# A two-stage mixture-of-experts kernel: seven of the 39 expert tiles get fixed widths from 112 down to 16 tokens

## What is computed

```python
def _L0_ffn_ref(hidden_states, Wr, W1, b1, W2, b2):
    x = hidden_states.reshape(b * s, d)
    router_logits = x @ Wr
    router_probs = jax.nn.softmax(router_logits, axis=-1)
    expert_idx = jnp.argmax(router_probs, axis=-1)
    p_max = jnp.max(router_probs, axis=-1, keepdims=True)
    def expert_mlp(w1, bb1, w2, bb2):
        h = jax.nn.gelu(x @ w1 + bb1, approximate=False)
        return h @ w2 + bb2
    outs = jax.vmap(expert_mlp)(W1, b1, W2, b2)
    onehot = jax.nn.one_hot(expert_idx, e, dtype=x.dtype)
    out = p_max * jnp.einsum('te,etd->td', onehot, outs)
...
x = x + 0.5 * _L0_ffn_ref(_layernorm(x), ...)
x = x + _L0_attn_ref(_layernorm(x), ...)      # h = a_disc * h + B_disc @ u; y = Re(C @ h)
x = x + 0.5 * _L0_ffn_ref(_layernorm(x), ...)
```

## Time and profile before

| | before |
|---|---|
| median of 3 runs | 636.2 us (635.69 to 638.94) |
| the profiled execution: its time, its span | 638.26 us, 636.5 us |
| busy: PE, PEld, DVE, ACT, POOL | 89%, 81%, 74%, 66%, 44% of the span |
| chain that ended last: PE, DVE, ACT | 76%, 12%, 4% of the span |
| L1104 (product 1), L1121 to L1123 (product 2) in that chain | 32%, 33% |
| first matmul of `ffn(1)` and of `ffn(2)` | at 99.0 us and at 414.0 us |
| last matmul of each | ends at 319.1 us and at 631.3 us |
| mean granted clock of PE | 0.991 |

### The profile page before, as it was taken

One profiled execution on the slowest core, in us unless ns is written; L12 is line 12 of the kernel. 1 busy time (PEld: TensorE's weight loads), 2 busy tenths in 40 slices (PEclk: granted clock), 3 DMA queues, 4 the chain that ended last, 5 costly groups with the idle time before them and its releaser, 6 DMA issues.

```text
span 636.5 us, 18503 instructions
## 1 busy us (share of the span) xinstructions
PE 565.4 (89%) x6476; PEld 518.6 (81%) x6476; DVE 473.1 (74%) x981; ACT 419.5 (66%) x966; POOL 280.3 (44%) x309
## 2 busy tenths in 40 slices
PE   5992118999998999999998988789999999999996
PEld 5991008999997999999956766689999999999996
DVE  6578995888888888888718997756677666666674
ACT  3697985767766676666625763277666676776662
POOL 0040055555455555554135113346555555555522
PEclk9999999999999999999999998899999999999999
DMA  8999021111121111121063114112111111111210
GB/s 270 368 377 324 5 82 35 52 38 53 40 51 44 39 49 50 50 52 37 19 191 109 66 67 138 49 36 61 38 51 52 50 49 50 47 42 51 44 33 1
DMA packets 34872, 51.93 MB, mean 82 GB/s; under 512 B 6747, under 2 KB 27933, under 8 KB 34528
## 3 DMA queue, kind: packets, MB, share of 16 engines
q1 hardware_dynamic: 24800, 31.93, 14.8%
q0 software_dynamic: 9984, 18.83, 11.0%
HBM read 37.98 MB, written 14.59 MB: 83 GB/s over the span
## 4 chain that ended last, share of the span: by engine, by line
PE 76%; DVE 12%; issue 4%; ACT 4%; DMA 2%; POOL 1%; SPq 0%; POOLq 0%; DVEq 0%; ACTq 0%
PE banks L1104 32%; PE banks L1123 11%; PE banks L1121 11%; PE banks L1122 11%; PE banks L1039 4%; DVE weights_arena L968 3%; PE banks L1080 3%; PE banks L1011 2%; ACT weights_arena L449 2%; DVE weights_arena L965 1%; DVE weights_arena L949 1%; ACT weights_arena L440 1%; DVE weights_arena L633 1%; DVE weights_arena L977 1%; PE banks L1017 1%
## 5 line engine op out<-in xcount | busy, mean ns | idle before, releaser
L523 ACT ACTIVATE weights_arena<-banks,b1t,inv 128x128 f32<-128x128 f32 x624 | 226.7, 469 | 37.5 <-PE banks L1104 37.4
L1104 PE MATMUL banks<-weights_arena 128*128 128x128 f16 x3744 | 222.1, 219 | 3.3 <-DVE weights_arena L825 2.0
L1104 PEld LDWEIGHTS banks<-weights_arena 128*128 x3744 | 215.1, 98 | 6.1 <-issue 5.3
L1123 PE MATMUL banks<-weights_arena 128*128 x624 | 170.1, 273 | 0.0
L1121 PE MATMUL banks<-weights_arena 128*128 x624 | 170.1, 273 | 0.0
L1122 PE MATMUL banks<-weights_arena 128*128 x624 | 170.1, 273 | 0.0
L836 DVE TENSOR_SCALAR weights_arena<-weights_arena,hscale 128x512 f16<-128x512 f32 x156 | 78.2, 501 | 58.1 <-ACT weights_arena L523 57.3
L839 DVE SCALAR_TENSOR_TENSOR weights_arena<-weights_arena,hscale 128x512 f16<-128x512 f32 x156 | 117.2, 752 | 5.6
L508 ACT ACTIVATE weights_arena<-banks,xscale 128x256 f16<-128x256 f32 x78 | 37.1, 476 | 98.0 <-PE banks L1080 95.7
L362 POOL DMA_INDIRECT recf<-records,sorti x78 | 85.5, 1097 | 23.8 <-issue 23.8
L368 POOL DMA_INDIRECT x_after_ffn<-weights_arena,sorti x39 | 40.0, 1025 | 89.6 <-DVE weights_arena L859 82.7
(11 more groups left out here) (201 smaller groups left out, 620.1 us busy)
## 6 DMA issues: line engine op xcount, KB each, us to landing
weights_arena<-L_ffn_W SPq DMA_DIRECT2D x16, 1024.0 KB, 12.6
weights_arena<-x_after_ffn SPq DMA_DIRECT2D x8, 516.0 KB, 7.4
weights_arena<-L_attn_u SPq DMA_DIRECT2D x8, 512.0 KB, 10.1
x_after_ssm<-weights_arena SPq DMA_DIRECT2D x8, 512.0 KB, 2.9
weights_arena<-L_ffn_b SPq DMA_DIRECT2D x2, 1024.0 KB, 5.3
recf<-records,sorti POOLq DMA_INDIRECT x78, 2.7
weights_arena<-L_attn_u,sorti POOLq DMA_INDIRECT x39, 3.2
x_after_ffn<-weights_arena,sorti POOLq DMA_INDIRECT x39, 2.6
```

Of the source, the lines that this page charges most:

```text
L523: last = act.activation(hb[q % 2][:, f, :], src, ACT.Gelu, bias=b1t[:, bass.ds(e * FC + f, 1)], scale=inv1[:, bass.ds(e, 1)])
L1104: last = pe.matmul(acc[:, f * P:(f + 1) * P], weights[wpart * DC + d], xts[q % 2][:, xpart, d, :], start=(n == 0), stop=(n == 5))
L1123: last = pe.matmul(acc, hs[q % 2][:, 1, f, :], high, start=False, stop=(f == FC - 1))
```

## The change

Seven of the 39 tiles, q = 32 to 38, get a fixed width of `width(q) = 16 * (39 - q)`: 112, 96, 80, 64, 48, 32 and 16 tokens. Their transposes, products, gelus, splits, results, gathers and scatters take only so many tokens. They hold the least filled last tiles of the experts, the least filled of all in the last place used. With M tiles in use, the k-th least filled last tile (k from 0) goes to place M - 1 - k if that is 32 or more; the eight experts' gaps add up to 128 (M - 32), so that it always fits. The tiles with 128 rows, the full ones and the fuller last ones, take places 0 to 31 in the experts' order.

To rank them, `route_count` gets more instructions on DVE (the gaps, `key`, a comparison of all pairs, `rank`, `place_of`, `partial`, `limit`, and two tables of tile places against experts). POOL gets `tile_slots`, seven instructions that make of these the number `vid` that the sorted order gave to each place. `route_tiles` compares with `vid_h` instead of a constant list, and so waits for POOL (`vids`). The sum of tiles (`tend`) moves from `route_owners` to `route_count`.

Three things move besides. In phase 2 the first two groups of `route_rows` stand ahead of `route_tiles`. `second_norm` gets its first half in the recurrence's chunk 5. And `turn_tile(1)`, which stood behind `product1(0)`, stands ahead of it in phase 1 and between its halves in phase 2.

```diff
+        def width(q):
+
+            return P if q < NJ else STEP * (NT - q)
...
+            def tile_slots(ph):
+
+                pool.wait_ge(S[ph]["slots"], 2)
+                parts = over_experts[:, NJ:NTE, :]
+                chain.link(pool.tensor_tensor(parts, parts, tend.unsqueeze(1).to_broadcast([P, NTE - NJ, E]), ALU.mult))
+                for n in (4, 2, 1):
+                    chain.link(pool.tensor_tensor(over_experts[:, :, 0:n], over_experts[:, :, 0:n],
+                                                  over_experts[:, :, n:2 * n], ALU.add))
+                pool.tensor_tensor(vid[:, 0:NJ], over_experts[:, 0:NJ, 0], iota_r[:, 0:NJ], ALU.add)
+                chain.link(pool.tensor_scalar(vid[:, NJ:NTE], over_experts[:, NJ:NTE, 0], -1.0, None, ALU.add))
+                pool.tensor_scalar(vid_h, vid, BIG / P, None, ALU.add).then_inc(S[ph]["vids"], 1)
...
+                if c == NC - 3:
+                    pool.wait_ge(s_sq, NC // 2)
+                    second_norm(slice(0, NJ // 2))
             pool.wait_ge(s_sq, NC - 1)
-            second_norm(slice(0, NJ - CT))
+            second_norm(slice(NJ // 2, NJ - CT))
...
-                            last = act.activation(hb[q % 2][:, f, :], src, ACT.Gelu,
+                            last = act.activation(hb[q % 2][:, f, 0:width(q)], src, ACT.Gelu,
...
-                link(dve.tensor_scalar(tend.bitcast(I32), tiles.bitcast(I32), 7, None, ALU.arith_shift_right))
-                link(dve.scalar_tensor_tensor(base, tend.bitcast(I32), float(P), cnt, ALU.mult, ALU.subtract))
-                link(dve.tensor_tensor(total[:, 1:E, 0], total[:, 1:E, 0], base[:, 0:E - 1], ALU.add))
+                link(dve.tensor_scalar(tiles_i.bitcast(I32), tiles.bitcast(I32), 7, None, ALU.arith_shift_right))
+                link(dve.scalar_tensor_tensor(slack, tiles_i.bitcast(I32), float(P), cnt, ALU.mult, ALU.subtract))
+                dve.tensor_copy(tiles, tiles_i.bitcast(I32))
+                link(dve.scalar_tensor_tensor(key, slack, float(E), rev[:], ALU.mult, ALU.add))
+                dve.tensor_tensor(total[:, 1:E, 0], total[:, 1:E, 0], slack[:, 0:E - 1], ALU.add)
+                dve.tensor_tensor_scan(tend, one[:].to_broadcast([P, E]), tiles, 0.0, ALU.mult, ALU.add)
+                larger = view(12288, E, E)
+                link(dve.tensor_tensor(larger, key.unsqueeze(1).to_broadcast([P, E, E]),
+                                       key.unsqueeze(2).to_broadcast([P, E, E]), ALU.is_gt))
+                link(dve.tensor_reduce(rank, larger, AX, ALU.add))
+                dve.tensor_scalar(place_of, rank, -1.0, tend[:, E - 1:E], ALU.mult, ALU.add)
+                link(dve.tensor_scalar(partial, rank, float(NJ), tend[:, E - 1:E], ALU.add, ALU.is_lt))
+                link(dve.tensor_tensor_scan(passed, one[:].to_broadcast([P, E]), partial, -64.0, ALU.mult, ALU.add))
+                link(dve.tensor_tensor(passed, tend, passed, ALU.subtract))
+                link(dve.scalar_tensor_tensor(limit, partial, -64.0, passed, ALU.mult, ALU.add))
...
+                dve.tensor_tensor(over_experts[:, NJ:NTE, :], per_slot(iota_r[:, NJ + 1:NTE + 1], NTE - NJ),
+                                  per_expert(place_of, NTE - NJ), ALU.is_equal).then_inc(s["slots"], 1)
+                dve.tensor_tensor(over_experts[:, 0:NJ, :], per_slot(iota_r[:, 0:NJ], NJ), per_expert(limit, NJ),
+                                  ALU.is_ge).then_inc(s["slots"], 1)
...
+                dve.wait_ge(S[ph]["vids"], 1)
...
             route_count(2)
+            route_places(2)
+            route_rows(2, 0)
+            route_rows(2, 1)
             route_tiles(2)
             route_odds(2)
-            for g in range(NJ // GR):
-                route_rows(2, g)
+            route_rows(2, 2)
+            route_rows(2, 3)
...
-                                        last = pe.matmul(acc[:, f * P:(f + 1) * P], weights[wpart * DC + d],
-                                                         xts[q % 2][:, xpart, d, :], start=(n == 0), stop=(n == 5))
+                                        last = pe.matmul(acc[:, f * P:f * P + n_cols], weights[wpart * DC + d],
+                                                         xts[q % 2][:, xpart, d, 0:n_cols], start=(n == 0), stop=(n == 5))
...
-                            pe.matmul(acc, hs[q % 2][:, 0, f, :], high, start=(f == 0), stop=False)
+                            pe.matmul(acc, hs[q % 2][:, 0, f, of], high, start=(f == 0), stop=False)
...
-                product1(0, w)
-                turn_tile(1)
+                if ph == 1:
+                    turn_tile(1)
+                product1(0, w, meanwhile=1 if ph == 2 else None)
```

90 lines of the change are left out of this document (54 added, 36 removed).

## The result

| | before | after |
|---|---|---|
| median (15 runs each, in turns) | 636.47 us | 630.44 us |
| ratio, 95% interval | | 0.991 (0.9881 to 0.994) |
| the profiled execution: time, span | 638.26, 636.5 us | 628.32, 626.4 us |

What follows compares the result with a forecast made beforehand. Only PE's time was taken to count inside the tile loops, with weight preparation and routing ahead of them; -0.15 - 7.2 - 0.3 + 3.3 - 7.2 - 0.3 = -11.85 us, from 636.2 to 624.3 us, range 620 to 632.

Steps and rivals of the forecast that it cites:

- The end of the second loop: Last scatter of the loop, 16 rows instead of 128: 0.3 us saved, between 0 and 1.
- Product 1: First product of the seven narrow tiles on PE: 7.4 us saved less 0.2 for the sequencer, 7.2 a phase (5.2 to 7.8).
- the two laws: Product 1's matmul price: by width with floor 25 ns, or straight line from 25 to 55.8; saving 7.8 or 7.0 us.
- The turn and product 2: Narrow tiles' transposes and second product on PE: no gain; product 2 keeps 109 ns a matmul and 2.62 us.
- Rivals A and B: Product 1 bound by its loads, 638.7 us (7%); product 2's narrow loads standing ahead of its matmuls, 642.3 us (8%).
- The ranking ahead of the first loop: Added DVE instructions in route_count delay ACT and DVE by 2.0 us, less 0.4 in route_owners: net +1.65 us.
- The start of the first loop: Turning tile 1 before product 1 of tile 0 lets tile 1's product 1 follow at once: -1.8 us.
- The routing of phase 2: Ahead of the second loop: DVE's ranking +2.1 us and its wait for POOL +1.0.
- the wait for POOL: DVE's tile table in phase 2's routing waits for POOL's vids: 0 to 3 us, taken as 1.0.
- PE's clock behind the longer gap: PE's longer idle before phase 2's routing matmuls leaves them slower: 0 to 0.7 us, taken as 0.2.
- The turn in phase 2: Tile 1's turn moved into product 1 of tile 0: gain 0, since norm(2) still waits for its gather.
- C: Rival: POOL holds up phase 2's routing, or the clock stays at 1.2 GHz beyond it: +3 to +6 us, 627 to 630; 15%.

Runs made afterwards that it cites:

- e3: The changed kernel with every gather moving 128 rows again, scatters still narrow; 628.57 us, 0.9841 of the kernel before.
- e7: The changed kernel with all scatters at 128 rows and gathers narrow in phase 2 alone; executed once for its trace, 662.79 us.
- e17: The changed kernel with compute narrow but all gathers and scatters at 128 rows; 621.97 us for 637.72 of the kernel before, 0.9779.
- e18: The kernel before with only the earlier turn of tile 1, no ranking, all widths 128; 0.9947 of the kernel before.
- e10: The changed kernel with compute narrow, all gathers and scatters at 128 rows, on a slower chip; 652.89 us, 0.991 of the kernel before.
- e9: The changed kernel as it is, run again on a slower chip; 663.15 us, 1.0056 of the kernel before (658.76 us).
- e12: Narrow compute, all DMAs 128 rows except the last two tiles' token-row gathers (208 rows fewer); executed once, 656.21 us.
- e5: The changed kernel with compute narrow, all gathers and scatters at 128 rows, on a slower chip; 655.4 us of 659.12, 0.9933.
- e11: The kernel before with only the earlier turn of tile 1, on a slower chip; 0.9998 of the kernel before.

## Why the prediction was wrong, step by step

- **The end of the second loop: the step that failed.** The prediction took 0.3 us off for a scatter of 16 rows, between 0 and 1, and looked at nothing behind it. The landing of the last scatter came 0.06 us sooner; POOL's DRAIN behind it made the end 8.4 us later, and it was the narrow gathers that made the DRAIN long (e3, e7), for which the sum had no term at all. The range of this step held no loss. The trace of before had the row to ask about: a DRAIN of 3.25 us that closes the queue which issued all indirect DMAs, and ends 0.62 us after SP is through. Its price with narrow DMAs wasn't to be had from before. But that they gain 0.3 us, 1 at the most, and that no row shows their bad end, was known, and speaks for leaving them full. e3 and e17 show the rest of the sum without it.
- **Product 1, forecast -7.2 a phase:** -6.74 in both. By the starts, the seven products 1 save 7.3 us (2.68 down to 2.36, 2.04, 1.73, 1.41, 1.30, 1.29, 1.29), close to the middle of the two laws. From start to start the matmuls follow the first of them (49, 42, 36, 30 ns for 112 to 64 columns, then 25.6), and the floor of 25 was near. The rest, 0.6 for the 0.2 taken, is mostly not in product 1: from product 2 of the tile with 112 columns on, the step from its last matmul to what follows takes 0.20 us for 0.11, five times a phase. What lengthens it isn't shown.
- **The turn and product 2, forecast 0:** right, 109 ns a matmul with 32 and with 16 stationary columns. The Trainium skill's TensorE: Matmul & The Clock Gate, Weight-path perf modes, has the fast load of weights only for 128 weights. The trace agrees: a load of 112 columns is recorded at 130 ns, one of 128 at 98; from 112 down the loads get shorter by 6 to 7 ns for every 16 columns, to 90 ns at 16. The 130 ns are more than the 93 ns that the prediction had estimated for 112 columns by its LDWEIGHTS section, and more than the 109 ns between two matmuls, but the loads overlap, one starting every 0.11 us, and stayed beside the matmuls. Rivals A and B have fallen.
- **The ranking ahead of the first loop, +1.65:** +1.69. ACT waits 2.10 us for expert 4's scales (`[2.10 <-DVE wscale L655]`), so there was no slack to hide it.
- **The start of the first loop, -1.8:** -2.0.
- **The routing of phase 2, +3.1:** +2.24. DVE's share, 2.1, was right; the wait for POOL, 0 to 3 and taken as 1.0, is 0. POOL needed 3.07 us for what I had put at 2.0 to 6.1 (389.21 to 392.28), and the cover was 3.4, for the 3.5 worked out. PE's clock behind the longer gap:

```profile
396.00:398.00 2.00, 2.00 (x16) 2.00 (x17) 1.79 (x12) 0.69 (x2) 0.29 (x1) 0.50 0.11 33
398.00:400.00 2.00, 2.00 (x12) 2.00 (x11) 1.11 (x4) 0.00 (x0) 1.69 (x2) 0.50 0.18 47
400.00:402.00 2.00, 1.41 (x8) 1.22 (x7) 0.00 (x0) 0.57 (x1) 1.39 (x3) 0.74 0.08 20
```

  These are windows of after, with the busy time of PE, PEld, DVE, ACT and POOL, then the granted clock, DMA share and GB/s. It is 0.50, 1.2 GHz, for the routing's matmuls up to 400, and full by product 1; +0.11 us for the 0.2 taken.
- **The turn in phase 2, 0:** -1.77. I had read `norm(2)` as held by its gather, since it waited for it before. That wait was real but not what set product 1 of tile 1: with tile 1 turned sooner, the gather lands in time for the turn of tile 2 behind product 1 of tile 0. In e18, without the ranking, it is -1.1.
- **The sum without the DRAIN:** the twelve stretches give -4.6, so -13.0 without its +8.4; e17 measured -14.1 (on another chip; its interval is 3.4 us to either side). The forecast's -11.85 was near for all but the last instruction.
- **The range** (620 to 632) held 630.4, by the spare room made for C and for losses in product 1. That it held is no merit of the reasons: what filled it was none of these.

## What to carry to other kernels

When DMAs of GpSimd are changed, look behind the last of them: a program ends with its slowest queue, and the closing DRAIN is part of the time though no line of the kernel asks for it. Narrow the compute where it is on the path, and leave the transfers as they are where they are hidden anyway: full gathers and scatters were worth 8 to 10 us more here (8.5 by the stretches of e17 and after, 10.3 by the medians of e10 and e9), and on a third chip 7, not clear of noise. And measure a gain that rests on the pace of very short instructions on more than one chip: the same change was 0.988 and 0.991 on two and 1.004 to 1.006 on two others.

## What was not expected of the hardware

- POOL's DRAIN at the end of a program takes 3.0 to 3.2 us, or 10.8 to 11.4, by what its gathers moved in the last loop (e12, between them, had 3.95). 32 rows fewer decide (448 left out: 3.2; 480: 10.8), but whether as a count of rows or because they are a gather of records isn't shown.
- Once in each loop of 117 indirect DMAs POOL stands for 2.2 to 2.4 us ahead of one of them, with no releaser in the profile; fewer rows move it later. Whether stop and DRAIN are the same housekeeping isn't shown, only that in the last loop there was either the one or the long other.
- On three chips PE stopped inside product 1 for 10 to 16 us in all (e5, e9, e10, e11), in pieces of up to 1.8 us, and at the starts of both loops above all. Most pieces fell on the step that issues a load and a matmul every 56 ns or less, but not all: product 2, with 109 ns, had 2.2 us of them in e10.
- Behind such stops PE's granted clock fell to 0.50 (e9: from 427.9 to 438.1 and from 629.3 to 632.7), and matmuls of product 2 started every 0.21 us for 0.11.
- A float16 stationary operand of 112 columns takes longer to load than one of 128 (130 ns recorded for 98), and with 256 moving columns neither shows in the pace of the matmuls (109 ns).
